# Cross-attention weights turned on VectorE in blocks of 32, and context products in four row groups

## What is computed

```python
q = rmsnorm((hidden @ Wq).reshape(B, Sq, H, D), gq)
k = rmsnorm((ctx @ Wk).reshape(B, Skv, H, D), gk)
v = (ctx @ Wv).reshape(B, Skv, H, D)
attn = softmax(einsum('bqhd,bkhd->bhqk', q, k) * scale)
out = einsum('bhqk,bkhd->bqhd', attn, v).reshape(B, Sq, H * D) @ Wo
...
x = x + tanh(g_xattn) * cross(layernorm(x), ctx)
x = x + tanh(g_ffn) * ffn(layernorm(x))     # ffn: rmsnorm, self-attention, rmsnorm, experts
```

## Time and profile before

| what | value |
|---|---|
| time, median of 3 runs | 643.88 us (643.67 to 643.96) |
| the profiled execution | 643.71 us |
| its span, first to last instruction | 641.8 us |
| TensorE clock granted, mean | 0.999 |
| busy: PE, DVE, ACT, POOL | 633.0, 460.7, 318.0, 252.6 us |
| first cross scores / first self scores / first chunk output | 14.50 / 199.45 / 424.12 us |

### The profile page before, as it was taken

One profiled execution on the slowest core, in us unless ns is written; L12 is line 12 of the kernel. 1 busy time (PEld: TensorE's weight loads), 2 busy tenths in 40 slices (PEclk: granted clock), 3 DMA queues, 4 the chain that ended last, 5 costly groups with the idle time before them and its releaser, 6 DMA issues.

```text
span 641.8 us, 16518 instructions
## 1 busy us (share of the span) xinstructions
PE 633.0 (99%) x6400; PEld 553.5 (86%) x6400; DVE 460.7 (72%) x881; ACT 318.0 (50%) x667; POOL 252.6 (39%) x336
## 2 busy tenths in 40 slices
PE   8999999999999999999999999999999999999997
PEld 6787888878788999899999999888879888888886
DVE  5868877897885776876677788755566977555556
ACT  6766666667653334333344333354467444444443
POOL 3221121212222533343352454445544755554553
PEclk9999999999999999999999999999999999999999
DMA  7522121110011232222221231113332232333332
GB/s 232 178 79 72 51 81 46 29 49 26 27 40 45 81 100 86 66 67 67 67 75 59 80 104 51 34 40 101 91 89 75 83 111 79 98 98 98 86 96 88
DMA packets 36016, 50.19 MB, mean 78 GB/s; under 512 B 4080, under 2 KB 23024, under 8 KB 35952
## 3 DMA queue, kind: packets, MB, share of 16 engines
q1 hardware_dynamic: 35376, 48.81, 25.7%
q10 hardware_dynamic: 576, 0.48, 0.2%
HBM read 48.22 MB, written 1.05 MB: 77 GB/s over the span
## 4 chain that ended last, share of the span: by engine, by line
PE 91%; DVE 6%; ACT 1%; issue 1%; DMA 1%; SPq 0%; DVEq 0%; ACTq 0%
PE acc L558 25%; PE bank_q L531 15%; PE bank_k L531 15%; PE bank_v L531 8%; PE bank_v L644 7%; PE bank_s L531 5%; PE bank_s L698 3%; PE bank_p L736 2%; PE bank_p L719 2%; PE bank_t L706 2%; PE bank_s L688 2%; PE bank_p L673 1%; PE bank_k L654 1%; PE bank_q L665 1%; DVE pv_lo L1328 1%
## 5 line engine op out<-in xcount | busy, mean ns | idle before, releaser
L558 PE MATMUL acc<-wo_hi,pv_hi 128*128 128x256 f32 x328 | 93.2, 284 | 1.5 <-DVE pv_lo L1463 1.5
L558 PE MATMUL acc<-wo_lo,pv_hi 128*128 128x256 f32 x328 | 92.9, 283 | 0.0
L558 PE MATMUL acc<-wo_hi,pv_lo 128*128 128x256 f32 x328 | 92.0, 281 | 0.0
L1619 POOL TENSOR_TENSOR wq_lo<-raw_a,wq_hi 128x256 fp32r<-128x256 f32 x32 | 23.4, 734 | 125.5 <-DVE wq_hi L1400 125.5
L558 PEld LDWEIGHTS acc<-wo_hi,pv_hi 128*128 128x128 f32 x328 | 61.5, 188 | 5.7 <-issue 2.6
L1619 POOL TENSOR_TENSOR wq_lo<-raw_m,wq_hi 128x256 fp32r<-128x256 f32 x50 | 40.2, 803 | 62.5 <-DVE wq_hi L1419 61.1
L558 PEld LDWEIGHTS acc<-wo_lo,pv_hi 128*128 128x128 f32 x328 | 61.6, 188 | 2.3
L558 PEld LDWEIGHTS acc<-wo_hi,pv_lo 128*128 128x128 f32 x328 | 62.3, 190 | 0.0
L1463 DVE TENSOR_TENSOR pv_lo<-raw_a,pv_hi 128x512 fp32r<-128x512 f32 (+1 forms) x51 | 37.1, 729 | 32.7 <-ACT pv_hi L1080 32.5
L531 PE MATMUL bank_q<-xt_hi,wq_hi 128*128 128x512 f32 x144 | 60.1, 418 | 0.0
L1080 ACT ACTIVATE pv_hi<-raw_a 128x512 fp32r<-128x512 f32 (+1 forms) x51 | 31.7, 624 | 56.4 <-DVE raw_a L1458 53.1
(11 more groups left out here) (223 smaller groups left out, 1885.4 us busy)
## 6 DMA issues: line engine op xcount, KB each, us to landing
raw_m<-in_chunk_m SPq DMA_DIRECT2D x50, 256.0 KB, 2.7
raw_a<-in_head_a SPq DMA_DIRECT2D x48, 192.0 KB, 2.9
raw_b<-in_head_b SPq DMA_DIRECT2D x32, 256.0 KB, 3.1
raw_m<-in_chunk_m SPq DMA_DIRECT2D x50, 128.0 KB, 2.1
raw_v<-in_pair_v SPq DMA_DIRECT2D x16, 256.0 KB, 2.8
raw_b<-in_head_b SPq DMA_DIRECT2D x32, 128.0 KB, 2.1
xs<-in_x SPq DMA_DIRECT2D x6, 128.0 KB, 3.3
out<-xs SPq DMA_DIRECT2D x3, 256.0 KB, 2.4
```

The lines of the kernel that those rows point to most:

```text
L558: last = nc.tensor.matmul(acc[t // 2][:, (t % 2) * D:(t % 2 + 1) * D], w[:, tok], m, start=begins and n == 0, stop=True, skip_group_check= ...
L1619: nc.gpsimd.tensor_tensor(lo, raw, hi, ALU.subtract).then_inc(signal, 1)
```

## The change

1. The weights are turned by one VectorE transpose in blocks of 32x32 (`turn_weights`), straight from `attn` to `rows_t`. TensorE's `turn_attn` and ScalarE's `take_rows` leave the cross pairs. With blocks of 32 the keys of one sequence lie in two column blocks of the same 32 partitions, so `context_values` makes 16 products of 32 keys by 128 columns, in four row groups and four banks, two of them added up in a bank. The context is laid out for it (same bytes, one load).
2. `pv_hi` and `pv_lo` are made in four pieces, one for each bank.
3. The four banks need room: the first cross keys are projected into bank_s, so that projection waits for "raw"; the second ones into bank_k wait for the first quarter of pv_lo. The second queries are taken by ScalarE (`qt_1`). `split_value_out` and the wait for it move.
4. Ahead of the self-attention both value projections stand together.
5. The token pieces of the second cross half, and of the experts in the chunks, are cut: rough, refine, centre for norm; refine_root and apply for scale. A new slot 2 lies between `subtract_max` and `normalise`; slot 1 moves ahead of `split_value_out`. Both token halves are awaited ahead of `norm_k`.
6. The logits are made in four column groups of 32 tokens.

```diff
-    beside_pairs("a", 0, ("x", 1), stats=(pairs - 5, 1), norm=(pairs - 4, 1), turn=(pairs - 3, 0))
-    for kind, half in (("a", 1), ("b", 0)):
-        beside_pairs(kind, half, ("y", half != 1), stats=(1, 1), norm=(2, 1), sums=(3, 0), root=(3, 1), scale=(4, 1),
-                     turn=(5, 0))
+    beside_pairs("a", 0, ("x", 1), stats=(pairs - 5, 2), norm=(pairs - 4, 1), turn=(pairs - 3, 0))
+    beside_pairs("a", 1, ("y", 0), stats=(1, 2), rough=(1, 1), refine=(2, 2), centre=(2, 1), sums=(3, 0), root=(3, 1),
+                 refine_root=(4, 2), apply=(4, 1), turn=(5, 0))
+    beside_pairs("b", 0, ("y", 1), stats=(1, 1), norm=(2, 1), sums=(3, 0), root=(3, 1), scale=(4, 1), turn=(5, 0))
...
-    experts = "sums root scale turn copy logits equals ties better ranks best - weights spread"
+    experts = "sums root refine_root apply turn copy logits equals ties better ranks best weights spread"
...
+        def context_bank(u, j):
+            return ((bank_k, bank_p, bank_t, bank_v) if u.deferred else (bank_v, bank_s, bank_p, bank_t))[j]
+        def context_of(u, j):
+            return context_bank(u, j)[:, 0:HT // 2].rearrange("p (h n q) -> p h n q", h=2, q=SEQ)
+        def key_bank(u, h):
+            return (bank_s, bank_k)[h] if u.kind == "a" else bank_k
...
             def scores(u):
-                pe.wait_ge(stage["qt"], u.of(1))
                 pe.wait_ge(stage["kt"], u.of(1))
                 if u.kind == "a":
+                    pe.wait_ge(A["qt_1"], u.n)
...
             def context_values(u):
-                for n in range(NT):
-                    at = (u.half * NT + n) * C
-                    for r in range(SPB):
-                        rows = slice(r * SEQ, (r + 1) * SEQ)
-                        last = nc.tensor.matmul(by_tile(value_bank(r)[:])[:, :, n, :], ctx_sb[rows, at:at + C],
-                                                rows_t[rows, n], start=True, stop=True)
+                turned = rows_t[:].rearrange("p t h q -> p (t h q)").rearrange("p (b n k q) -> p n k b q", n=2, k=2, q=GROUP)
+                for n in range(2):
+                    for k in range(2):
+                        at = ((u.half * 2 + n) * 2 + k) * C
+                        for j in range(QUADS):
+                            rows = slice(j * GROUP, (j + 1) * GROUP)
+                            last = nc.tensor.matmul(context_of(u, j)[:, :, n, :], ctx_sb[rows, at:at + C],
+                                                    turned[rows, n, k], start=k == 0, stop=k == 1)
...
# logits, TensorE
-                            last = nc.tensor.matmul(turn_banks(u)[1][:, t * E:(t + 1) * E], xt[:, k, t * P:(t + 1) * P],
+                            for j in range(0, P, GROUP):
+                                last = nc.tensor.matmul(turn_banks(u)[1][j:j + GROUP, t * E:(t + 1) * E],
+                                                        xt[:, k, t * P + j:t * P + j + GROUP],
...
# cross_pair, TensorE
                     pe.wait_ge(A["ln_k"], u.n)
+                    if prev.weighs_values:
+                        pe.wait_ge(A["vo_lo"], prev.n)
                     context_values(prev)
                 if nxt.kind == "a":
-                    if prev and prev.weighs_values:
-                        pe.wait_ge(A["vo_lo"], prev.n)
+                    pe.wait_ge(A["raw"], u.n)
                     project_keys(nxt, 0)
                 pe.wait_ge(A["ln_q"], u.n)
                 project_queries(nxt, 0)
+                if prev:
+                    pe.wait_ge(A["pv_lo"], QUADS * (prev.n - 1) + 1)
                 project_keys(nxt, int(nxt.kind == "a"))
...
-                    release(held[:1])
+                    release(held)
                     if not prev:
                         pe.wait_ge(A["ln_k"], u.n)
-                        norm_k(nxt)
-                    turn_attn(u)
-                    release(held[1:])
-                    if prev:
-                        norm_k(nxt)
+                    norm_k(nxt)
                 else:
                     project_queries(nxt, 1)
-                    turn_attn(u)
-                    project_values(nxt, False)
                     context_values(u)
                     project_keys(nxt, 1)
+                    pe.wait_ge(A["pv_lo"], QUADS * (u.n - 1) + 2)
+                    project_values(nxt, False)
                     project_values(nxt, True)
...
# ScalarE
+            def take_second_queries(u):
+                nc.scalar.activation(qt[:, 1], query_bank(u, 1)[:], ACT.Copy, scale=gqk[:, 0:1]).then_inc(A["qt_1"], 1)
...
-                for r in range(SPB):
-                    nc.scalar.activation(by_row(pv_hi[:], r), value_bank(r)[:].rearrange("p (h n) -> p h n", h=2),
-                                         ACT.Copy).then_inc(A["pv_hi"], 1)
+                for j in range(QUADS):
+                    nc.scalar.activation(quads(pv_hi[:])[:, :, :, j, :], context_of(u, j), ACT.Copy).then_inc(A["pv_hi"], 1)
...
                 else:
-                    take_v(nxt, False)
                     take_context_values(u)
                     take_k(nxt, 1)
+                    take_v(nxt, False)
...
# VectorE
+            def turn_weights(u):
+                if u.n > 1:
+                    v.wait_ge(A["pv_done"], u.n - 1)
+                v.wait_ge(A["norm"], u.n)
+                nc.vector.transpose(rows_t[:].rearrange("p n h q -> p (n h q)"), attn[:].rearrange("p g k -> p (g k)"))\
+                    .then_inc(A["attn_t"], 1)
...
             def cross_pair(u):
-                if prev:
+                hurried = prev and prev.very_first
+                if hurried:
+                    split_context_values(prev)
+                take_max(u)
+                if prev and not hurried:
                     split_context_values(prev)
                 subtract_max(u)
...
+                prepare_piece(*piece_at(u, 2), u)
                 normalise(u)
                 if nxt.kind == "a":
                     take_q(nxt, 0)
+                turn_weights(u)
...
-                take_q(nxt, 1)
+                if nxt.kind == "b":
+                    take_q(nxt, 1)
                 split_queries(after, 1, nxt)
...
+                prepare_piece(*piece_at(u, 1), u)
                 if u.weighs_values:
                     split_value_out(u)
-                prepare_piece(*piece_at(u, 1), u)
...
# chunk, VectorE: these pieces run behind split_hidden
-                with_scalar = piece_at(u)[0] in ("turn", "logits", "spread")
+                with_scalar = piece_at(u)[0] in ("turn", "logits", "spread", "refine_root", "apply")
```

More of the change, by code:

```diff
@@ L333, in flamingo_layer @@
         A = stage_sems("a", "wq_hi wq_lo wk_hi wk_lo q_done k_done sq_q sq_k qt kt scores raw scaled max "
-                       "sub exp sum inv norm t_done attn_t vo_done vo_hi vo_lo ssk_done ssq_done ssq ln_q "
+                       "sub exp sum inv norm attn_t vo_done vo_hi vo_lo ssk_done ssq_done ssq ln_q qt_1 "
                        "ln_k r_k r_q pv_done pv_hi pv_lo wo_done")
@@ L566, in output @@
                 if u.kind == "a":
-                    pe.wait_ge(A["pv_lo"], u.of(1))
+                    pe.wait_ge(A["pv_lo"], QUADS * u.n)
                     if u.weighs_values:
@@ L615, in project_queries, with project_keys @@
                 project(query_bank(u, h), wq_hi[h], wq_lo[h], tokens_hi(u), tokens_lo(u)).then_inc(stage["q_done"], 1)
-            def project_keys(u, h, bank=bank_k):
-                stage = stages[u.kind]
+            def project_keys(u, h):
+                stage, bank = stages[u.kind], key_bank(u, h)
                 pe.wait_ge(stage["wk_lo"], u.of(h))
-                if h and bank is bank_k:
-                    pe.wait_ge(stage["kt"], u.of(0))
+                if h and u.kind == "b":
+                    pe.wait_ge(B["kt"], u.of(0))
                 if u.kind == "a":
@@ L702, in turn_attn @@
             def turn_attn(u):
-                stage = stages[u.kind]
-                pe.wait_ge(stage["norm"], u.n)
+                pe.wait_ge(B["norm"], u.n)
                 for b in range(G // 2):
@@ L707, in turn_attn @@
                                                attn[:, 2 * b:2 * b + 2, :].rearrange("p t k -> p (t k)"), ident)
-                last.then_inc(stage["t_done"], 1)
+                last.then_inc(B["t_done"], 1)
             def context_values(u):
@@ L909, in _ @@
             for h in range(2):
-                project_keys(start, h, (bank_k, bank_s)[h])
+                project_keys(start, h)
             project_first_queries(start)
@@ L963, in prepare @@
                 piece, step = piece_at(u, slot)
-                if piece == "norm" and step[0] != "x":
+                if piece == "rough" or piece == "norm" and step[0] != "x":
                     rough_root(step)
@@ L991, in square_q, with take_k @@
                 nc.scalar.activation(sq_q[:, h], query_bank(u, h)[:], ACT.Square, scale=SCALE).then_inc(A["sq_q"], 1)
-            def take_k(u, h, bank=bank_k):
```

(24 more changed lines are left out.)

25 lines of the change are left out of this document (10 added, 15 removed).

## The result

The changed kernel takes 637.63 us, median of 4 runs (637.52 to 637.76); the kernel before, on the same chip, 643.92 (643.67 to 643.99). The ratio is 0.9903, 95% interval 0.9886 to 0.9920: faster by 6.3 us where 11.4 were forecast, and 0.6 above the forecast's range. The profiled execution took 637.76 and its span is 636.0, so 5.8 us are to be found in the trace (641.8 before).

What follows compares the result with a forecast made beforehand. TensorE, busy 633.0 of 641.8 us, was taken as the bound. Savings of 8.4, 3.3, 1.5 and 1.8 us less added waits gave -11.4, so 643.8 became 632.4, range 630.0 to 637.0.

Steps and rivals of the forecast that it cites:

- (1): Cross pairs: taking turn_attn out of TensorE's queue saves 15 x 0.53 + 0.4 = 8.4 us.
- (2): TensorE's waits for late VectorE: new places for token pieces return 3.3 us in pairs, 1.5 in the chunks.
- (7): First keys into bank_s wait for raw: hidden by 0.2 us in quiet pairs; first two pairs together +1.0.
- (3): Logits in four column groups: 0.8 us for 1.70, so 0.9 saved, twice: 1.8 us.
- (4): Context products as 32 instructions of 32 rows: four row groups overlap fully, no change from 1.10 us.
- C: Rival: four row groups reach only three quarters of full overlap, +4 us, 636.4; chance 0.08.
- D: Rival: row groups run only two at a time, +14 us, 646.5, slower; chance 0.04.
- (5): VectorE in cross pairs: transpose 0.72 us; quartered pv_lo steps 0.33 each, ready 0.2 before the output: hidden.
- (6): ScalarE's quartered pv_hi and qt_1 copy: hidden, except 0.5 us in the pair of the sums, 0.25 in the next.
- rival B: VectorE becomes the bound of the cross pairs: TensorE waits some 0.3 in 13 pairs, +4 us, 636.4; chance 0.16.
- (8): Token turn, second half: norm_k waits for both xt_lo, behind VectorE's transpose, +0.6 us.
- (9): Cross to self: second value projection waits for ScalarE's copy of the first, first keys for pv_lo: +1.05 us.

Runs made afterwards that it cites:

- all of them together: Changed kernel with slot 1 ahead of the casts, new order to self, first keys in bank_t, gate cast before refine_root, xt_lo before the transpose: 633.87 us.

## Why the prediction was right and wrong

The numbers in brackets are those of the prediction's parts; where no run is named, lengths are read between the same marks before and after.

(1) The turn: right in kind, too large. 15 x 0.53 was taken as the step from turn_attn to norm_k. Of it 0.45 and 0.41 came back in a quiet pair, 6.4 us in place of 8.0. The missing 0.1 shows one step earlier: value_out ahead of norm_k steps on in 0.95 for 0.86, in the second half the output in 1.53 for 1.44. Those are the steps from full tiles to column groups of 32. Before, turn_attn was that neighbour and had this 0.09 within its 0.53; the self pair's 0.39, which I had in hand, is the price without it. "Mode switching requires drain", the Trainium skill says of this ("TensorEngine Tiling (Array Packing)", Key Properties), without a price. The rows agree at 0.09 us, and the run with the logits alone has it once more, where nothing but the next group's tiling changes: the last full-tile matmul ahead of the logits steps on in 0.20 for 0.12 at 362.29, and in 0.32 for 0.23 at 488.69. That full tiles ahead of column groups of 32 cost this much is shown, then; that it is a drain, and not the shorter weight loads behind it, is not.

(2) The waits: this is the step that failed. The small operations in slot 2 were hidden, as said, and the statistics gave their 1.1. But "the four wide ones (1.14, as in the row at 478.06) go behind the last wq_hi, where it is idle 1.19 in the first half" took their price from a row in which GpSimd was idle, and put them at the one place in the pair where it is not: the idle 1.19 itself, up to 57.40 in the kernel before, has GpSimd's subtractions beside it (56.02 to 57.63). In the changed kernel each group of four takes 2.5 us, and the three together cost TensorE 2.5: 0.73, 0.79 and 0.98 in the three pairs, and 2.3 by the median. That TensorE feels it is the other half of the step: with the keys behind raw, which (7) had said would show "at once" where VectorE is late, there was no slack left, as there is in the kernel with the pieces alone. The Trainium skill has the rule: the "shared port pair" of VectorE and GpSimd is held "for the full instruction", and the one that loses it "fully blocks" ("SBUF — State Buffer", Terms). The rows agree in kind: 1.14 against 2.52, 0.16 against 0.72. They don't show a full block. In the group at 133.91 the single operations end 0.15 us behind one of GpSimd's four each, while one by itself steps on in 0.32 (in the run that holds GpSimd back), and both engines' work, 1.38 and 2.4 us, is done in 2.57. How much of an instruction can run beside GpSimd's stays open.

The chunks: -1.5 was forecast. The chunk of the cut became 0.82 shorter (4.90 us for 5.72), and 0.4 is what the run with the cut undone shows in the whole. The wait of 1.29 did go; 0.47 took its place, since the five small operations make the wq_hi cast late, and GpSimd with it.

(3) The logits: 0.67 for the 0.8 taken. Their step is 1.03 shorter; with the 0.09 of the switch ahead of them, 0.92 was saved in the first half (the pair is 14.79 us for 15.71) and 0.95 in the chunks, where 0.9 each was forecast, and 0.7 was given back behind. "The weights that turn_attn wants behind it are there before" looked one step far; what came back came over the seven chunks behind.

(4) The context products: right. 32 instructions in 1.11 us; row groups of 32 overlap in full, rivals C and D are out. The 3.07 times of the Trainium skill would have shown as 1.35 ("TensorE: Matmul & The Clock Gate", Part 3, an estimate). Its figure is for 512 moving columns; with the 128 of this kernel the measured row decides against it.

(5) and (6) Right. The transpose takes 0.70 (0.72 taken), a quarter of pv_lo 0.41 and steps in 0.34 (0.33 taken), qt_1 0.68 (0.6 taken). VectorE is not the bound of a quiet pair, so rival B is out as it was priced; the run with the turn alone shows how near it was. The pair of the sums is 10.87 with the collision out of the way, 0.63 over a quiet one (0.75 taken).

(7) The first two pairs are 9.02 and 11.92 for 8.36 and 12.10; less the 0.9 that quiet pairs lost, they cost 1.4 where 1.0 was taken. In quiet pairs raw is in time, and the 0.2 for it did not appear.

(8) The token turn: without the collision its pair is 11.65, which is 10.24 + 0.8 for the transposes + 0.6, as taken. (9) The way to the self pairs is 16.25 for 15.24; since the sum took 0.4 off there for the turn, the waits cost 1.4 where 1.05 was taken. The run that changes the order and the banks gave 1.1 back.

Short of the forecast, then: 1.5 (turn) + 2.5 (collision) + 0.7 (cut in the chunks) + 0.7 (behind the logits) + 0.4 (first pairs) + 0.35 (to self) - 0.2 (raw) - 0.1 (logits) - 0.1 (sums) = 5.75, against 5.1 measured by the medians (11.4 less 6.3) and 5.6 by the spans (11.4 less 5.8). Runs of their own stand behind the collision (2.3 us came back), the cut in the chunks (worth 0.4, by which its term would be 1.1) and what goes back behind the logits (0.67); the other terms are read from the traces.

Open stays how far the turn alone could go: its waits were not repaired one by one. Nor was it tried to move the norm of the keys so that fewer switches of tiling are left.

## What to carry to other kernels

A gap on an engine is not free time for every operation: before work is moved into a gap of VectorE, read what GpSimd does in it, and take the price from a row with the same neighbour. Its sign in a trace is a small operation that takes several times what its like takes elsewhere, as 0.66 us for 0.16 at 137.73 in the kernel before. An edit that takes work off the bounding engine also takes cover off all the others; the new first wait stands as near as the first instruction that needs them, here 2.1 us behind the scores in place of 5. Price a removed step by what its neighbours do without it, not by its step between two neighbours that differ in kind.

## What the runs showed of the hardware

- Four VectorE operations of 128x256 with a scalar, SBUF to SBUF, take 1.10 to 1.38 us alone and 2.51 to 2.53 beside four of GpSimd's subtractions; a 128x4 one 0.16 alone and, beside one, up to 0.72, with its end at GpSimd's (468.60, 469.36, 470.05 in the run of all of them together). GpSimd's own 128x256 take 0.73 to 0.79 beside the first; behind the gate cast, beside VectorE's operations of 128x512 with two inputs, one takes 1.11 (469.29).
- Matmuls of 32 rows and 128 moving columns, in four row groups and four banks: 32 in 1.11 us, the time of 16 with 64 rows.
- 64 matmuls with 32 weight columns and 16 moving ones, in four column groups, take 0.67 us; the same work in 16 matmuls of 128 weight columns 1.70.
- A full-tile matmul steps on 0.08 to 0.09 us later when a group of 128x32 tiles follows it: 0.20 for 0.12 and 0.32 for 0.23 ahead of the logits, 0.95 for 0.86 for value_out ahead of norm_k.
